# Attention and three residual layers on one core: weight pieces and one pair's operands in another order, GpSimd's rows of unit 8 behind the last low parts, two smaller last stores

## What is computed

```python
q, k, v = x @ Wq, x @ Wk, x @ Wv
attn = softmax(q @ k.T * 512 ** -0.5)
attn_out = (attn @ v) @ Wp + bp
cms = gelu(attn_out @ cW1 + cb1) @ cW2 + cb2 + one_hot(code)
mod = gelu(concat(attn_out, cms) @ mW1 + mb1) @ mW2 + mb2
y = clip(x + cms + mod, 0, 1)
for l in (1, 2, 3):                      # e = index of the sequence, 1 or 2
    h = gelu(y @ W_down[l][e] + b_down[l][e])
    z = y + h @ W_up[l][e] + b_up[l][e]
    y = (z - mean(z)) / sqrt(var(z) + 1e-5) * gamma[l][e] + beta[l][e]
```

## Time and profile before

| | |
|---|---|
| median of three runs | 1178.15 us (1177.11 to 1178.33) |
| the profiled execution | 1176.59 us |
| its span, first to last instruction | 1174.5 us |
| TensorE (PE) busy | 1162.6 us, 99% |
| VectorE (DVE) busy | 754.1 us, 64% |
| ScalarE (ACT) busy | 528.6 us, 45% |
| GpSimd (POOL) busy | 174.1 us, 15% |
| DMA | 251.76 MB, mean 214 GB/s |

### The profile page before, as it was taken

One profiled execution on the slowest core, in us unless ns is written; L12 is line 12 of the kernel. 1 busy time (PEld: TensorE's weight loads), 2 busy tenths in 40 slices (PEclk: granted clock), 3 DMA queues, 4 the chain that ended last, 5 costly groups with the idle time before them and its releaser, 6 DMA issues.

```text
span 1174.5 us, 15531 instructions
## 1 busy us (share of the span) xinstructions
PE 1162.6 (99%) x5260; PEld 963.6 (82%) x5260; DVE 754.1 (64%) x1336; ACT 528.6 (45%) x961; POOL 174.1 (15%) x154
## 2 busy tenths in 40 slices
PE   9999999999999999999999999999999999999997
PEld 8888887888888788888888888888888888888885
DVE  6345386776767865656567676685555545767787
ACT  5434354564543534343434535442231313357886
POOL 1331230000000000000000000000000000358995
PEclk9999999999999999999999999999999999999999
DMA  5754553546644726363698789756767678946655
GB/s 219 274 197 158 183 179 120 177 143 225 216 159 174 262 97 245 105 242 117 226 406 302 247 293 312 205 197 195 230 193 230 192 231 289 356 162 210 223 186 197
DMA packets 113332, 251.76 MB, mean 214 GB/s; under 512 B 13396, under 2 KB 13396, under 8 KB 109926
## 3 DMA queue, kind: packets, MB, share of 16 engines
q1 hardware_dynamic: 113110, 250.52, 62.8%
q10 hardware_dynamic: 144, 0.26, 0.1%
HBM read 155.30 MB, written 95.43 MB: 213 GB/s over the span
## 4 chain that ended last, share of the span: by engine, by line
PE 93%; DVE 3%; ACT 2%; issue 1%; POOL 1%; DMA 1%; DVEq 0%; POOLq 0%; ACTq 0%
PE psum L757 89%; PE psum L1025 1%; PE psum L970 1%; DVE c_op L1635 1%; PE psum L791 1%; DVE a_op L1440 1%; PE psum L811 0%; ACT z L1333 0%; ACT res L1368 0%; PE psum L806 0%; PE psum L822 0%; DMA prep<-wdu_dram 0%; DVE ring L1525 0%; DMA wdu_split<-prep 0%; ACT yT L1356 0%
## 5 line engine op out<-in xcount | busy, mean ns | idle before, releaser
L757 PE MATMUL psum<-a_op,ring 128*128 128x512 f32 x1344 | 316.5, 389 | 0.3 <-DVE w_t L1567 0.3
L757 PEld LDWEIGHTS psum<-a_op,ring 128*128 128x128 f32 x1344 | 252.1, 188 | 53.2 <-DVE w_t L1567 0.8
L757 PE MATMUL psum<-g_hl,w_hl 128*128 128x512 f32 x1152 | 263.4, 389 | 0.0
L757 PEld LDWEIGHTS psum<-g_hl,w_hl 128*128 128x128 f32 x1152 | 216.1, 188 | 45.3 <-DVE g L1581 0.4
L757 PE MATMUL psum<-c_op,ring 128*128 128x512 f32 x672 | 163.3, 390 | 0.4 <-DVE c_op L1635 0.3
L757 PEld LDWEIGHTS psum<-c_op,ring 128*128 128x128 f32 x672 | 125.8, 188 | 27.8 <-DVE c_op L1635 1.8
L1180 ACT ACTIVATE g<-g,sm 128x512 f32<-128x512 f32 x96 | 69.5, 724 | 137.4 <-DVE g L1573 66.7
L1593 DVE TENSOR_TENSOR g_hl<-g,g_hl 128x512 fp32r<-128x512 f32 x96 | 66.1, 689 | 51.3 <-ACT g_hl L1203 50.4
L1964 POOL MEMSET acc_u<- 128x1024 f32 x1 | 1.0, 955 | 591.7 <-DVE w_hl L1586 591.7
L1160 ACT CAST ring<-asum 128x256 fp32r<-128x256 f32 x96 | 38.5, 404 | 103.9 <-PE psum L757 75.5
L1203 ACT CAST g_hl<-g 128x512 fp32r<-128x512 f32 x96 | 58.5, 618 | 50.9 <-PE psum L757 50.9
(11 more groups left out here) (156 smaller groups left out, 1583.9 us busy)
## 6 DMA issues: line engine op xcount, KB each, us to landing
up_operands<-ring SPq DMA_DIRECT2D x168, 256.0 KB, 2.8
ring<-up_operands SPq DMA_DIRECT2D x168, 256.0 KB, 3.0
wdu_split<-prep SPq DMA_DIRECT2D x36, 512.0 KB, 3.0
down_operands<-stage SPq DMA_DIRECT2D x56, 256.0 KB, 4.9
ring<-down_operands SPq DMA_DIRECT2D x56, 256.0 KB, 2.9
rawp<-up_w_dram SPq DMA_DIRECT2D x24, 512.0 KB, 4.5
wraw<-dn_w_dram SPq DMA_DIRECT2D x48, 256.0 KB, 3.8
wu<-wdu_split SPq DMA_DIRECT2D x12, 1024.0 KB, 5.5
```

The costliest lines, as they stand in the source:

```text
L757: ins = nc.tensor.matmul(ps, lw(el), rw(er), start=first and i == 0, stop=last and i == 2, skip_group_check=skip)
```

## The change

Three things, in the order of the program's time.

In the attention loop the copies of the pieces get other places on ScalarE: piece 2 ahead of x's high parts, pieces 3 and 4 after them (in the third pass each behind one of the pair's operands), and pieces 5 to 8 one behind each tile of uT, where they were one ahead of the first tile and one behind each of the first three. In the third pass P7's high part comes first of the four sums' operands, and P4's last, behind the whole of uT; VectorE makes the low parts of P7 and P5 one step later, P6's behind the second tile of uT, P4's behind the fourth.

In the last stage GpSimd, after the roots of unit 9, waits until both low parts of h of unit 11 are made (`t_hlo` at 12 * MT), then does two of the remaining row operations of unit 8, the roots of unit 10, and then the last three.

The last 128x512 of output 3 are stored in two halves of 128x256, the first by SP ahead of the two last row tiles, the second by ScalarE.

```diff
@@ block.sync
             sp.wait_ge(t_yf, turned(11) + 2)
             sp.dma_start(out[3, :, 0, :], res[:, 3, 0, :]).then_inc(s_out, 16)
+            sp.wait_ge(t_yf, turned(11) + 3)
+            sp.dma_start(out[3, :, 1, 0:2 * P], res[:, 3, 1, 0:2 * P]).then_inc(s_out, 16)
             for i in LAST_ROWS:
...
-            sp.wait_ge(s_out, 16 * 8)
+            sp.wait_ge(s_out, 16 * 9)
@@ block.scalar
                 def after_v(m):
                     if m < 2:
-                        piece(0, m)
+                        piece_hi(b + 1, m)
...
                 def after_u(m):
-                    piece(2 * PSLOT, m)
-                    if b == 2 and m == 0:
-                        attention_hi(0, P4, after_sum=4, after_lo=PROD - 1)
+                    piece_hi(b + 1, PHASE - DT + m)
+                    if b == 2 and m == DT - 1:
+                        attention_hi(0, P4, after_sum=4, after_lo=PROD - 3)
...
                 hi_jobs(n + JV + DT, LOW, lambda m: v_n[:, 0, m, :], tiles=(3,))
+                piece_hi(b + 1, 2)

                 x_hi_parts(b + 1)
-                piece(0, 2)
                 if b == 2:
                     attention_hi(0, P2)
-                for m in range(PSLOT):
-                    piece(PSLOT, m)
+                    attention_hi(0, P7, after_sum=1)
+                piece_hi(b + 1, 3)
                 if b == 2:
-                    attention_hi(0, P7, after_sum=1)
                     attention_hi(0, P5, after_sum=2)
+                piece_hi(b + 1, 4)
+                if b == 2:
                     attention_hi(0, P6, after_sum=3)
                 hi_jobs(n + JU, HIGH, lambda m: uT[:, 0, m, :], scale=SCALE, after=after_u)
...
-            nc.scalar.dma_start(out[3, :, 1, :], res[:, 3, 1, :]).then_inc(s_out, 16)
+            nc.scalar.dma_start(out[3, :, 1, 2 * P:], res[:, 3, 1, 2 * P:]).then_inc(s_out, 16)
@@ block.vector
                         attention_sum(0, (P7, P5, P6, P4)[m])
-                        if m > 0:
-                            attention_lo(0, (P7, P5, P6)[m - 1])
+                        if m >= 2:
+                            attention_lo(0, (P7, P5)[m - 2])

                 def after_u(m):
-                    if b == 2 and m == 0:
-                        attention_lo(0, P4)
+                    if b == 2 and m in (1, 3):
+                        attention_lo(0, (P6, P4)[m // 2])
@@ block.gpsimd
-            for s in range(14):
-                if 3 <= s < 12:
+            for s in range(11):
+                if 3 <= s:
...
+            rows_scaled(8, 0)
+            rows_scaled(8, 1)
+            rows_shifted(8, 0)
+            rstd_of(9)
+            pool.wait_ge(t_hlo, 12 * MT)
+            rows_shifted(8, 1)
+            rows_scaled(8, 2)
+            rstd_of(10)
+            rows_scaled(8, 3)
+            rows_shifted(8, 2)
+            rows_shifted(8, 3)
+            rstd_of(11)
```

More of the change, by code:

```diff
@@ L1098, in _ @@
                 n = b * PER
-                def piece(c, m):
-                    if m < PSLOT:
-                        piece_hi(b + 1, c + m)
                 def after_v(m):
                     if m < 2:
-                        piece(0, m)
+                        piece_hi(b + 1, m)
                     if b == 2 and m < 2:
```

## The result

The changed kernel takes **1175.66 us** (median of 20 runs, 1174.77 to 1176.79). The kernel before, run beside it, takes 1178.38 us (20 runs, 1177.11 to 1180.11). The ratio is 0.9977 with a 95% interval of 0.9971 to 0.9983: 2.7 us or 0.23% faster. The forecast was 1176.3 us, 1.8 us faster. The time lies in the range given, but just over the line of 0.2%, where I had given "faster" 0.26 and "same" 0.69; the interval holds that line.

A forecast was written before the change was run, and what follows sets the result against it. TensorE, busy 1162.6 of 1174.5 us, was taken to bound the kernel, with the output drain at the end. Attention -2.33 plus drain +0.5 gave -1.8 us: 1178.15 to 1176.3 us, range 1175.1 to 1178.0.

The forecast's parts named there:

- The attention part, -2.33: Third pass of the sequence loop: the new order removes TensorE's whole stall for uT's low part, -2.33 us.
- P7's high part no longer stands behind pieces 3 to 5: ScalarE, attention loop: P7's high part waits only for its sum and ends near 162, not 166.5.
- The tile times: VectorE, third pass: uT's four low parts end at about 169.3, 171.1, 173.8 and 176.6, the last with 0.7 us slack.
- The row work of unit 8: Last stage: GpSimd's wait frees unit 9's factors and unit 11's low parts; unit 10's statistics come 1.7 us sooner.
- The drain, +0.5: End of kernel: outputs 0 and 1 are stored 5 us later; the gapless 10.5 us drain ends 0.5 us later.
- The 0.6 us of compute: Last stage: ScalarE's last chain starts 0.6 us sooner, at 1160.4 for 1160.98, but the drain hides this.
- No issue sets the end: Last stores: with DMA engines busy throughout, the order and time of SP's issues do not set the end.
- the smaller stores at 0: Output 3's last 256 KB as two 128 KB stores: 0 to 0.7 us more was possible, 0 taken.
- the tail wins too: Rival: GpSimd's rows end by 1161.9 and compute's 0.6 us count; -2.9 us, 1175.2 us, chance 0.18.
- The slower drain: Rival: final stores drain slower, by the skill's rule or packet cost; tail +1.2 to +1.7, about 1177.4 us, chance 0.11.
- caught behind the roots: Rival: unit 10's statistics are not sooner, output 0 waits longer; tail +3.2, 1179.0 us, chance 0.06.
- The sum, -1.8: Whole kernel: attention -2.33 plus tail +0.5 gives -1.8 us, so 1176.3 us on the median; chance 0.57.

The follow-up runs named there:

- kernel 9: The kernel before with only ScalarE's new attention order (pieces and P7 early; P4's high part stays behind uT's first tile): ratio 0.9974.
- kernel 10: The kernel before with only VectorE's new order of attention low parts, plus P4's copy on ScalarE moved last: ratio 0.9969.
- kernels 2: The kernel before with only GpSimd's new order in the last stage: ratio 1.0007.
- 4: The kernel before with the attention part and GpSimd's last-stage order, without the smaller stores: ratio 0.9981.
- 11: The changed kernel run again with no edit: ratio 0.9984 to the kernel before, median 1176.37 us.
- Kernels 5: The changed kernel without the stores of outputs 0 and 1: ratio 0.9961 to the kernel before.
- kernel 7: The changed kernel with two of GpSimd's last three row operations of unit 8 ahead of unit 10's roots: ratio 0.9962 to the kernel before, median 1174.12 us.
- kernel 8: The changed kernel with two row operations ahead of unit 10's roots and the last after unit 10's factors: ratio 0.9958 to the kernel before, median 1174.05 us.
- 12: The changed kernel with two row operations before unit 10's roots, the last after its factors, and the old last stores: 0.9960 to the kernel before, 1173.95 us.
- kernels 3: The kernel before with only the two smaller last stores: ratio 1.0002.
- kernels 1: The kernel before with only the attention-loop changes on ScalarE and VectorE: ratio 0.9976.
- 6: The kernel before with only the attention-loop changes, and without the stores of outputs 0 and 1: ratio 0.9969 to the kernel before.

## Why the prediction was right or wrong

- **The attention part, -2.33: right in size.** Measured -2.30 in the changed kernel, and -2.28 to -2.33 in every kernel with both orders, whatever its tail.
- **The reasons for it: half right.** "P7's high part no longer stands behind pieces 3 to 5" is enough to remove the stall (kernel 9, all but 0.2 us) but not needed (kernel 10). The stall wanted both at once: the high part late, and low parts and P4's copy in the way of uT. Undoing either cures it but for 0.2 us, and doing both gains no more than one. That P4's copy held ScalarE for 3.17 us in front of uT's second tile is missing from the prediction, which names VectorE's order alone for the late tiles.
- **The tile times: wrong on the way, right at the end.** The forecast had P7's and P5's low parts done by 168.7 (169.3 in this profile, which runs 0.58 us later here), at 1.15 us each. In the trace they took 2.32 and 2.31 us, beside GpSimd's low parts of pieces, P5's was done at 172.40, and the first two uT tiles started only at 172.33:

```profile
166.06 2.32 DVE L1438 TENSOR_TENSOR a_op<-a_t,a_op 128x1024 fp32r<-128x1024 f32 x1
...
170.09 2.31 DVE L1438 TENSOR_TENSOR a_op<-res,a_op 128x1024 fp32r<-128x1024 f32 x1
172.33 1.27 DVE L1402 SCALAR_TENSOR_TENSOR uT<-psum,uT 128x512 fp32r<-128x512 f32 x2
...
176.70 0.69 DVE L1402 SCALAR_TENSOR_TENSOR uT<-psum,uT 128x512 fp32r<-128x512 f32 x1 [1.36 <-ACT uT L1049]
```

  The last tile ends at 177.39, and TensorE wants it at 175.87 + 2.04 = 177.91: a slack of 0.5 us, where I had 0.7. The step that failed is the duration of a low part with GpSimd beside it, which rows of before had shown (P6's took 2.31 us there). The slack covered it: the first two tiles end at 173.60, and TensorE wants them from 175.87 on. The last tile is not held by it; it follows TensorE's own product.
- **The row work of unit 8: each step right.** Factors of unit 9 0.16 us (forecast 0.16), two low parts 1.29 (1.3), output 0 issued 5.92 us after the last up product (1162.85 in the old profile's time, 5.93 after its product at 1156.92), the factors of unit 10 1.14 (1.26).
- **The drain, +0.5: right in mechanism, 0.27 too small.** The tail grew by 0.77 us (0.67, 0.73 and 0.76 in kernels 2, 4 and 11). The drain took 10.6 to 10.7 us at a share of 0.99, not 10.5, and the program ended 1.1 us behind it, not 0.9. Kernels 5 and 7 show that the drain sets the end: take the bytes away, or start them 2.5 us sooner, and the tail falls by 1.25 and 1.28 us, with the compute chain as it was. The 0.6 us of compute that I had hidden under it were there too: ScalarE's normalisation of unit 10 starts 0.62 us sooner after c.
- **"No issue sets the end", the smaller stores at 0: nearly.** They cost 0.17 us alone and 0.12 in kernel 8 against 12. Behind a gap, the end comes 6.07 to 6.11 us after output 2's last issue with the split store (kernels 3, 5, 7, 8) and 5.87 to 5.96 without (before and kernels 1, 6, 9, 10, 12). No profile of one kind lies among the other's, so I take 0.1 to 0.2 us as shown.
- **The rivals.** That the tail wins too did not happen, but it was one order away: kernel 8 is that rival, at -1.07 us. The slower drain came in part, at the end of the window (374 GB/s from 1166.90 to 1172.50):

```profile
1166.90:1172.50 5.60, 0.00 (x0) 0.00 (x0) 1.07 (x2) 1.15 (x3) 0.00 (x0) 0.68 0.98 374
```

  Over the whole drain it was 392 GB/s, and the tail cost 0.77 us. The Trainium skill's rule in "DMA: Bandwidth & Descriptors", section "Where 436 GB/s comes from", of about 358 GB/s is not borne out by these stores, with one core at work: by it the tail was to cost an estimated 1.7 us. No output was caught behind the roots beyond the forecast.
- **The sum, -1.8: by the trace -1.45 to -1.55, by the runs -2.7 and -1.9.** In the trace the sum is off by 0.38 us: 0.27 in the tail, 0.03 in the attention part, 0.08 between b and c. The runs miss it on the other side, by 0.9 and 0.1 us, with a gain that no term of mine explains; that the time fell into the range is therefore in part luck. So is the side of 0.2%: 0.9977 lies on one, 0.9984 of the same kernel on the other.

What stays open: the gain of the medians is 0.5 to 1.7 us larger than the trace's net for all kernels with the attention change, where kernels 2 and 3 agree within 0.4. The profile of before, at 1176.59 us, is faster than every timed run of that kernel and has the earliest start a. Each timed run also has its span. For the kernel before the median span is 1176.2, 1176.85 and 1176.4 us in the three groups of runs beside kernels 1 to 4, 5 to 8 and 9 to 12, and its profile has 1174.5, 1.7 to 2.4 us less; for the other 13 the profile lies between 1.2 us below and 0.3 us above its own median. So it is the profile of before that is short, by more than the 1.4 us that starts a differ. The stall is no part of this: it is there at 2.26 and 2.45 us in kernels 3 and 2. What the rest is, one profile of before can't say.

## What to carry to other kernels

Before you delay an engine's work to free another, ask what transfer waits for it, and reckon the drain: the bytes still to be written, over the measured rate, from the first issue. As long as that leaves a gap, the delay is free (kernels 7 and 8 issue output 0 2.4 and 2.8 us later than before and have the shorter tails); past it, a later issue costs time (here 1.3 us for the last 2.5) that the compute gained here, 0.6 us, doesn't win back. Fill the other engine's idle stretch first (kernel 7), then delay. When you have two cures for one stall, try each alone: they may be one cure twice. And look at what each engine in the chain waits for, not only the last one: here a copy waited for a low part that it didn't need.

## What the runs showed of the hardware

- VectorE and GpSimd hold each other for a whole instruction, even when it is a tiny one that is held. The 128x4 factors take 0.15 us alone and 1.14 or 1.26 beside a row operation; in the changed kernel they end at 1158.66, and the GpSimd operation beside them (1157.34, 1.29 us) ends at 1158.63. The low parts of 128x1024 take 1.21 us alone and up to 2.32 beside GpSimd. GpSimd is held too: two of its row operations took 1.82 and 1.75 us beside VectorE's low parts in the kernel before (at 1151.89 and 1153.66), where undisturbed ones take 1.3. The Trainium skill has this in "SBUF — State Buffer", section "Who interferes with whom": a VectorE instruction with two inputs in SBUF contends with a GpSimd instruction that reads it, and one of them waits for the whole of the other. The trace agrees, with 1158.66 and 1158.63.
- 4.2 MB of stores ran at 392 GB/s without a gap, and at 404 GB/s in kernel 7's window. At the end of a drain the rate was lower: 366 GB/s before, 374 in the changed kernel, 358 in kernel 7.
- Between profiles time is lost or won ahead of the first product of x: 17.92 to 18.96 us among kernels 5 to 8, on one chip, and up to 1.4 us over all 14. Spans of single profiles can't be compared below that unless they are cut at a common instruction; cut so, the changed kernel's two profiles agree to 0.1 us.
